# Convolutions on four segments of 32 columns: 64x32 tiles for two filters, 32x32 tiles for the third, the average as one matmul

## The reference

```
for l in range(3):                       # kernels of 3x3, 5x5 and 7x7 taps, one filter per channel
    ctx = gelu(dwconv_same(ctx, k[l]))   # 'SAME' padding, feature_group_count = C
    ctx_all += ctx * gates[..., l:l+1]
ctx_global = gelu(mean(ctx, axis=(H, W)))
ctx_all += ctx_global * gates[..., 3:]
```

## Time and profile before

| | |
|---|---|
| median of 3 runs | 8685.42 us (8683.92 to 8726.74) |
| span of the profiled execution | 8678.4 us, 336810 instructions |
| TensorE busy (PE) | 7853.7 us, 90% |
| VectorE, ScalarE, GpSimd busy | 6360.4, 4495.5, 5624.9 us |
| granted TensorE clock | 9 tenths or more in all 40 slices |

### The profile page before, as it was taken

How to read it: one execution, slowest core, us unless ns; L and a number is a source line. 1 busy time by engine, 2 the same in 40 slices (tenths; PEclk the granted TensorE clock), 3 DMA queues, 4 the chain that set the end, 5 groups by cost and what they waited for, 6 DMA issues and landing times. The chain is left out here.

```text
span 8678.4 us, 336810 instructions
## 1 busy us (share of the span) xinstructions
PE 7853.7 (90%) x120363; PEld 5180.1 (60%) x120363; DVE 6360.4 (73%) x21127; ACT 4495.5 (52%) x12517; POOL 5624.9 (65%) x6959
## 2 busy tenths in 40 slices
PE   7999999979999999869989999997999788888888
PEld 6777777754444444447767766655777555555554
DVE  7999999979999999878857777777888422222222
ACT  5666666645655555559933333335666333333333
POOL 8888888868888888768812222225777544444444
PEclk9999999989999999989999999999999899999999
DMA  1222222211111111148855555538888222222221
GB/s 52 58 58 58 58 58 58 57 55 58 57 56 56 56 59 57 63 157 300 295 189 187 180 188 190 193 132 219 232 231 229 77 56 57 56 56 56 56 57 53
DMA packets 797829, 958.44 MB, mean 110 GB/s; under 512 B 323100, under 2 KB 661825, under 8 KB 773584
## 3 DMA queue, kind: packets, MB, share of 16 engines
q1 hardware_dynamic: 797264, 952.06, 35.9%
HBM read 574.81 MB, written 453.35 MB: 118 GB/s over the span
## 5 line engine op out<-in xcount | busy, mean ns | idle before, releaser
L991 PE MATMUL moe_pe_out<-moe_we,moe_xnT 128*128 128x512 f32 x3136 | 1482.0, 607 | 179.2 <-DVE moe_acc L885 172.3
L1595 PE MATMUL conv_pc<-conv_c,conv_toep 64*64 64x432 f32 (+1 forms) x12260 | 1356.3, 527 | 2.5 <-ACT conv_c L1497 2.5
L2314 ACT ACTIVATE rec_yT<-rec_ph 128x32 f32<-128x32 f32 x3136 | 618.3, 197 | 1242.5 <-PE rec_ph L2435 1242.5
L787 ACT ACTIVATE moe_scaled<-moe_pe_out,moe_gate 128x128 f32<-128x128 f32 x3136 | 892.0, 367 | 692.6 <-PE moe_pe_out L991 690.6
L991 PEld LDWEIGHTS moe_pe_out<-moe_we,moe_xnT 128*128 128x128 f32 x3136 | 546.8, 191 | 942.4 <-issue 940.9
L1452 POOL TENSOR_TENSOR conv_g<-conv_c,conv_gate 128x896 f32<-128x896 f32 x128 | 366.6, 2864 | 1123.8 <-DVE conv_out L1565 1086.2
L2361 DVE COPY rec_xT<-rec_pin 128x512 f32<-128x512 f32 x196 | 135.6, 692 | 1240.1 <-PE rec_pin L2407 1240.1
L1595 PEld LDWEIGHTS conv_pc<-conv_c,conv_toep 64*64 64x64 f32 (+1 forms) x12260 | 855.3, 133 | 310.9 <-issue 108.8
L2435 PE MATMUL rec_ph<-rec_yT,rec_vt 128*32 128x32 f32 x25080 | 844.5, 207 | 195.5 <-ACT rec_yT L2314 120.8
L307 POOL TENSOR_SCALAR att_xn<-att_xin,att_mv,att_rstd 128x128 f32<-128x128 f32 x1024 | 881.9, 871 | 54.1 <-POOL att_rstd L303 54.1
L2435 PEld LDWEIGHTS rec_ph<-rec_yT,rec_vt 128*32 128x32 f32 x25080 | 496.9, 108 | 646.9 <-ACT rec_yT L2314 608.9
(11 more groups left out here) (212 smaller groups left out, 19859.0 us busy)
## 6 DMA issues: line engine op xcount, KB each, us to landing
conv_toep<-rows_dram SPq DMA_DIRECT2D x32, 2304.0 KB, 13.7
c<-foc_cs SPq DMA_DIRECT2D x32, 1792.0 KB, 10.9
conv_cin<-c SPq DMA_DIRECT2D x32, 1792.0 KB, 10.2
ctx_all<-conv_out SPq DMA_DIRECT2D x32, 1792.0 KB, 6.5
att_xin<-x_windows SPq DMA_DIRECT2D x512, 98.0 KB
moe_xin<-x SPq DMA_DIRECT2D x112, 448.0 KB, 3.5
x<-moe_acc SPq DMA_DIRECT2D x112, 448.0 KB, 2.7
foc_xin<-x SPq DMA_DIRECT2D x32, 1568.0 KB, 8.3
```

What stands on the lines that cost most here:

```text
L787: ins = act.activation(scaled[:, b, e, :], pe_out[:, b, 1, e * C:(e + 1) * C], ACT.Identity, scale=g)
L991: pe.matmul(pe_out[:, b, half, :], xnT[:, n.slot(2), t, :], we[:, half * 4:half * 4 + 4, :].rearrange("d e c -> d (e c)"), start=True, sto ...
L1595: return pe.matmul(image_pairs(pc[k], half)[m0:m1, :, i0:i1], w, tile[r0:r1, images(half), i0 + away:i1 + away], start=start, stop=True, s ...
L2314: act.activation(yT[:, a, cs], ph[:, a, cs], ACT.Sigmoid).then_inc(moved, 1)
```

## The change

The 56 pixels of a row are held as two segments of 32 partitions, so that the 128 partitions are four segments (two rows, two segments each). Each segment owns 28 pixels.

- The input and the first filter's taps stay as they were. The second filter's input and output, and the third filter's input, hold pixels 0 to 31 in one segment and 24 to 55 in the other: the 8 pixels in the middle are computed twice. What the third filter needs for the 28 owned outputs of a segment then lies in that segment alone.
- `block_of` makes the first two filters as two matmuls of 64 rows by 32 columns each (8 tiles). The second filter's taps lie in a tile of their own, `toep2`, zeroed once by GpSimd, whose unused rows stay zero.
- `segment_of` makes the third filter as 32x32 matmuls (16 tiles) of 224 columns (8 images), into four PSUM banks `pc3`: the four row segments write to four different banks, and half of the output segments are swapped. `third_filter` is called twice, and the second call waits for the first.
- `average` is one matmul of the whole array, in the tail of a bank of the first filter, and waits for the gelu that reads this bank.
- The order of a channel is now: both filters' first halves, both second halves, the average, the whole third filter.
- The gelus of the first two filters lose their scale; the swapped gelu of the third is four pieces of 32 partitions.
- SP loads the gates and the gap mask in 12 small DMAs instead of 2, the taps in 5 instead of 1, and stores in 4 pieces of 28 partitions instead of 1.

The diff's core:

```diff
-        pc = [S.ps(f"pc{k}", [P, 2, BANK]) for k in range(3)]
-        pm = S.ps("pm", [P, BANK])
+        pc = [S.ps(f"pc{k}", [P, 2, BANK]) for k in range(2)]
+        pc3 = S.ps("pc3", [P, SETS, BANK])
+        pm = pc[0][:, 1, HALF * EVEN:HALF * EVEN + B]
...
+        def quad(row, half):
+            return slice(row * ROW + half * SEG, row * ROW + half * SEG + SEG)
...
+                for seg in range(2):
+                    o0 = m0 + seg * SEG
+                    ins = pe.matmul(image_pairs(pc[k], half)[o0:o0 + SEG, :, i0:i1], taps[:, at + seg * FROM:at + seg * FROM + SEG],
+                                    tile[:, images(half), i0 + away:i1 + away], start=start, stop=True, skip_group_check=True)
...
+            def segment_of(n, away, row, to_row, half, swapped, which, start):
+                s, ch = channel(n)
+                rows, outs = quad(row, half), quad(to_row, half ^ swapped)
...
+                return pe.matmul(pc3[outs, which, 0:EACH * EVEN].rearrange("p (b i) -> p b i", i=EVEN)[:, :, i0:i1],
+                                 toep[rows, s, ch, at:at + SEG],
+                                 c2[rows, n.slot(2), first_image:first_image + EACH, i0 + away:i1 + away],
+                                 start=start, stop=True, skip_group_check=True)
...
+            def third_filter(n, later):
+                for turn in range(4):
+                    for row, to_row in ((0, 0), (1, 1), (1, 0), (0, 1)):
+                        further = 2 if to_row > row else -2
+                        aways = (0, -1, 1, further) if row != to_row else (0, -1, 1)
+                        if turn == len(aways):
+                            continue
+                        for half in range(2):
+                            for swapped in range(2):
+                                ins = segment_of(n, aways[turn], row, to_row, half, swapped, 2 * swapped + (row ^ later),
+                                                 turn == 0 and not later)
+                return ins
+
+            def average(n):
+                hold(pe, pooled_part, n.val(1, 1), ticks)
+                pe.matmul(pm, ones[:], pooled[:], start=True, stop=True, skip_group_check=True).then_inc(averaged, 1)
...
                 if has1:
-                    ready(0, n + 2, first + 2)
-                    first_filter(n + 2, 0, 1, True)
+                    first_half(0, n + 2, first + 2)
                 if has2:
-                    ready(1, n + 1, first + 1)
-                    second_filter(n + 1, 0, 1, True).then_inc(firsts_made, 1)
-                if has3:
-                    ready(2, n, first)
-                    third_filter_on_own_rows(n)
...
+                    first_half(1, n + 1, first + 1)
+                if has1:
+                    second_half(0, n + 2)
+                if has2:
+                    second_half(1, n + 1)
+                if first >= 1:
+                    if has1:
+                        hold(pe, activated[0], n.val(1, 3), ticks)
+                    average(n - 1)
                 if has3:
-                    hold(pe, thirds_made, n.val(1, 1), ticks)
-                    third_filter_on_other_rows(n)
+                    ready(2, n, first)
+                    third_filter(n, 0).then_inc(thirds_half, 1)
+                    hold(pe, thirds_half, n.val(1, 1), ticks)
+                    third_filter(n, 1).then_inc(convolved[2], 1)
```

More of the change, by code:

```diff
@@ L1352, in convolution_stage @@
     N = C
+    SETS = 4
+    EACH = B // SETS
     HALF = B // 2
@@ L1418, in load @@
                     hold(sp, rows_made[s], g.turn(2, 48), ticks)
-                sp.dma_start(toep[:, s, :, :], dram(rows_dram, s * PER * P * T_ALL, [(T_ALL, P), (P * T_ALL, PER), (1, T_ALL)]))\
+                rows = s * PER * P * T_ALL
+                sp.dma_start(toep[:, s, :, :], dram(rows_dram, rows, [(T_ALL, P), (P * T_ALL, PER), (1, T_MAIN)]))\
                   .then_inc(toep_in[s], 16)
+                if first == 0:
+                    sp.wait_ge(zeroed, 2)
+                for row in range(2):
+                    for half in range(2):
+                        sp.dma_start(toep2[own(row, half), s, :, :],
+                                     dram(rows_dram, rows + (row * ROW + half * OWN) * T_ALL + T_MAIN,
+                                          [(T_ALL, OWN), (P * T_ALL, PER), (1, T_SIDE)])).then_inc(toep_in[s], 16)
             def step(n, first, last):
@@ L1578, in _, with channel @@
             pe.wait_ge(zeroed, 1)
[L1580 to L1589, removed]
+            LOW, HIGH = (0, ROW), (ROW, P)
+            def channel(n):
+                return Step(n.loop, U // PER, n.off // PER).slot(2), n.off % PER
@@ L1590, in block_of @@
+            def block_of(k, n, half, away, rows, outs, start=False):
+                s, ch = channel(n)
                 (r0, r1), (m0, m1) = rows, outs
+                tile = (cin[r0:r1, s, :, ch, :], c1[r0:r1, n.slot(4), :, :])[k]
+                taps = (toep, toep2)[k][r0:r1, s, ch, :]
+                at = FURTHEST[k] - P * away + m0
                 i0, i1 = max(0, -away), min(EVEN, EVEN - away)
-                w = toep[r0:r1, s, ch, at + m0:at + m1]
-                if k == 2 and half == 1:
-                    m0, m1 = ROW - m0, ROW - m0 + ROW
```

145 lines of the change are left out of this document (67 added, 78 removed).

## The result

The changed kernel takes 9161.53 us (median; 9147.53 to 9166.94), against 8706.06 us for the kernel before on the same chip. The ratio is 1.0535, with a 95% interval of 1.0511 to 1.056. (The four runs of the kernel before fall into two pairs, near 8685 and near 8727 us, and the quotient of the two medians is 1.0523.) It is 5% slower, and 9161 lies 316 us above the end of my range.

The account below looks back on a forecast made before the run. TensorE's array tiles were taken to bound the convolution stage. Per channel, 9.6 us of work and waits + 1.4 supply + 0.4 loop end = 11.4 us against 11.37, giving 8691, forecast as 8695 us; range 8475 to 8845.

Parts of the forecast that it names:

- What bounds the kernel before: Convolution stage: TensorE's array tiles bound it, busy 394.35 of 400 us, with 20.0 us of issue gaps at loop ends.
- First and second filter, 5.9 us: First two filters: 64 matmuls on eight tiles instead of 32 on four keep their array time, 5.9 us a channel.
- Third filter, 2.5 us: Third filter: 224 records on sixteen tiles at once take 2.5 us a channel instead of 5.0.
- Average and switches 0.3, waits 0.8: Per channel: three switches of tile shape around the average cost 0.3 us, newly exposed waits for other engines 0.8.
- Supply, +1.4 and 0.4 us: TensorE's instruction fetch: late packets, mainly in the third filter, add 1.4 us a channel, the loop's end 0.4.
- 3.2 us for a missing packet: Instruction fetch: a late packet costs the loop branch's median 3.446 us less 0.215 us for a resident loop's branch.
- the 0.6 in the upper bound: Instruction fetch: an amount added in the 2.3 us upper bound of the stall, (3.65-1.5) x 0.8 + 0.6.
- Loads hide, "below 9.5 they would not": SP's added DMAs: taps land 18 to 20 us after a group's end, hidden unless a channel falls below 9.5 us.
- The stage's start: Before the first channels: ten more small DMAs cost 4 to 8 us, some 5 come back; net +2 us.
- rival A: Convolution stage: the instruction fetch is hidden, 10.0 us a channel, 8510 us in all; chance 0.33.
- B: Third filter: instruction fetch costs more than the array gains, 12.3 us a channel, 8805 us in all; chance 0.20.
- C: Third filter: sixteen tiles do not overlap as eight do, 20 ns a record, 12.6 us a channel, 8845 us; chance 0.07.

Follow-up runs that it names:

- e9: The kernel before, with TensorE's program for the stage written out for all channels, without its loop of 8: 8658.7 us, ratio 0.9971.
- e1: The changed kernel with the filters reading constant tiles in SBUF and TensorE's loop body 2 channels instead of 8: 8713.4 us, ratio 1.0031.
- e3: e1 with the third filter's matmuls on 4 of their 8 images, same number of instructions: 8657.6 us, ratio 0.9961.
- e5: e1 with both operands of the third filter as constant bf16 tiles, two instructions a matmul instead of four: 8635.2 us, one run.
- e8: The kernel before with only the average changed to one 128x128 matmul: 8772.0 us, ratio 1.0084.
- e10: The changed kernel with TensorE's program for the stage written out, without its loop of 8: 9098.9 us, ratio 1.0474.

## Why the prediction was wrong

Two terms of the sum failed. The third filter's array time was put at 2.5 us a channel, as if sixteen tiles streamed without a break, and is 4.85. The supply of instructions was put at 1.4 + 0.4 us and takes 3.4. Term by term:

- **What bounds the kernel before**: right. e9 shows TensorE with no gap at all once the branch is gone, and its 25 us are the 20.0 of the earlier trace rows and a little more.
- **First and second filter, 5.9 us**: right, about 6.1 to the end of the last record when undisturbed (4635.51 to 4641.65 in e1).
- **Third filter, 2.5 us** (224 records x 0.179 / 16): this step failed. I tested whether records can start every 11 ns, and they do, but for 32 of them. Then 64 instructions are in flight and a tile waits for its own. 4.85 us. The bursts of the earlier trace rows could not show it: their records are short, on at most eight tiles.
- **Average and switches 0.3, waits 0.8**: 0.31 us from the average's start to the third filter's, and 0.15 us between the halves, in the undisturbed channels of e1. So the waits were put too high. The same average inside the old kernel costs 0.67.
- **Supply, +1.4 and 0.4 us**: this term failed too, in its size. The mechanism was right, with its packets (24 a loop, 384 in the stage), its place and its branch, but it costs 3.4 us a channel. The terms were 3.2 us for a missing packet, and one packet ahead. Two of the numbers behind them were loose: 250 of 452 instructions in 2.5 us last 1.4 us, not 1.5, and the 0.6 in the upper bound has no row. Shown: with the loads off the queues the loss falls from 3.4 to 1.5 us, so the price depends on traffic, and I had priced it at a row of the branch. Hardly counted: late blocks in filters 1 and 2 (up to 5.07 us at a time). Not counted at all: the granted clock, at 0.50 after such stops, at most 1.05 us a channel.
- **Loads hide, "below 9.5 they would not"**: the limit is 11.4 us in the long run, since SP's chain is a cycle and not only a lead time. Had rival A's 10.0 us come true for TensorE, the channels would have slowed to that. The stage's start was put at +2 us and is +10.
- **The rivals**: B (fetch) and C (sixteen tiles do not overlap) came true together. Their prices, 12.3 and 12.6, were each taken with the other absent; the stall of C was even made smaller. C's 20 ns a record was nearly exact (2.36 us for 112 is 21), and had a chance of 0.07. From the measured terms, the third filter's with the wait between its halves: 6.1 + 0.3 + 4.85 + 3.4 = 14.65 us, against 15.02. Most of the rest is e1's own branch after every second channel: e1 alternates between 11.24 and 11.76 us, so that its 11.55 is 0.3 above an undisturbed channel.

What stays open: why TensorE goes on only 2.5 us after a packet's start when the packet takes 1.1 to 1.2, and what in the loads delays the packet (the expansion of the taps, their load, or that of c0). That was not tried.

## What to carry to other kernels

Count instructions, not only array time: an fp32 matmul is four of them, TensorE held 64 in e1, e3 and e5, and beside loads a block of the program came every 3.7 us at the quickest and every 4.5 in the median. In this kernel smaller tiles would have paid only with one turn of all tiles well under 64 instructions (as in e5, where a channel could take 8.6 us), and with a block's instructions lasting longer than its arrival. Before a step is cut, price the next chain as a cycle (here SP's, 11.4 us a channel), and try the branch-free program: it gave the kernel before 0.3% (e9).

## What the runs showed of the hardware

- A body of 1,440 instructions stays with TensorE (no packet in 1200 us); one of about 2,030 does not, and costs a branch of 3.6 us (e8). Where the body stays, the branch takes 0.21 us (e1). Where between the two the limit lies was not tried.
- The Trainium skill ("Runtime: NRT & Kernel Launch", instruction fetch mechanics) says that crossing a block is mostly hidden, and that a taken branch breaks the fetch ahead. The first holds at one block per 10.7 us (e9, 111 packets in 1186 us, no idle time) and fails at one per 5 us (after, 16% idle); the second agrees with e9 and e10.
- Sixteen 32x32 fp32 tiles with 224 columns reach 112 records in 2.36 us, 21 ns each, hardly faster than four 64x64 tiles for the same data. In bf16, 56 in 0.76 us, 14 ns.
- One 128x128 matmul of 32 columns among 64x64 tiles costs 0.67 us more than four 64x64 ones (e8).
